# A fused Mamba block and mixture of experts on one core: the depthwise convolution of all four channel tiles as diagonal matmuls on TensorE, added onto a last tap that ScalarE writes into PSUM

## The chip, the cores and the metric

One core of one Trainium2 chip runs the whole kernel as one program. Times are device microseconds (us) of one execution. A timed figure is the median of several executions; the profile is of one further execution. The engines are named as in the profile: PE is TensorE, PEld its weight loads, DVE is VectorE, ACT is ScalarE, POOL is GpSimd, and SP issues the DMAs. L839 is line 839 of the kernel before.

## What is computed

The input has 8 sequences of 1024 tokens with 256 channels. Two layers follow each other, each inside a layer norm and a residual addition:

```
x = x + layernorm(mamba(layernorm(x)))
x = x + layernorm(moe(layernorm(x)))

mamba(x): xn = rms_norm(x) ; xb, z = split(xn @ in_proj_w)        # 256 -> 2 x 512
          xc = silu(causal_conv(xb, 4 taps, per channel) + conv_b)
          dt, B, C = split(xc @ x_proj_w) ; dt = softplus(dt @ dt_proj_w + dt_proj_b)
          h_t = exp(dt*A) * h_(t-1) + dt*B*xc ; y_t = sum_s C*h_t  # 512 channels x 16 states
          (y + xc*D) * silu(z) @ out_proj_w + residual
moe(x):   16 experts of width 128, the best 4 of them per token, within 2 of 4 groups
```

The part that matters here is the causal convolution: each of 512 channels has four weights of its own, and output `t` is `w0*x[t-3] + w1*x[t-2] + w2*x[t-1] + w3*x[t] + b`. All numbers are float32.

## The kernel before

**Chunks and groups.** The 8192 tokens are cut in 16 chunks of 512 tokens, two to a sequence. Channels lie on the 128 partitions, so the 512 inner channels make four tiles `m = 0..3`. The scan over 512 channels x 16 states of a chunk is cut in 16 groups, each of four scans (`beta`). The loop is `for p` over chunks -2 to 17 and `for g` over 16 groups (`groups()`), and every engine walks the same (p, g) in its own queue, in order. In pass p four stages run at once on different chunks: E (layer norm and transpose of chunk p+2), F (input projection, convolution, dt, B, C of chunk p+1), S (the scans of chunk p), and P with the experts (output projection, norms, routing of chunk p-1, then its experts, which begin ten groups later). E exists for 16 passes, F for p = -1 to 14, S for p = 0 to 15. The experts run beside the scans from group 10 of pass 1 on.

**One group on each engine.** DVE: the gate product of an expert (`expert_gate`, L995), scan 0 (L880), the up product (L1000), scans 1 to 3, then what the pass adds in this group, then `inputs` of the next group (L866). ACT: the exponentials `dA` of the scans (`decay`, L508, two banks, so that each waits for the scan two before it), `tanh` of an expert (L514), and the pass's own pieces between and behind them. PE: `add_states` (L448, L451), the expert's `gate` (L421) and `up` (L429), the fill of this group, `down` of an older expert (L439), and a second fill in some groups. `gate` of a group waits for DVE's gate product of the same group, which frees its bank (`m_v`); DVE's next gate product waits for `tanh`, which stands behind the decays of the next group's scans 0 and 1. POOL weighs experts (L759) and multiplies states by C (L769).

**The one shared bank.** All fills of the stages E, F and P go through a single PSUM bank, `FP`, in the fixed order of the list `FILLS`: PE fills it, ACT reads it, and PE's next fill waits for that read (`bank_free`, with the table `FREED_BY`). Input-projection fills are `b0..b3` and `z0..z3` (two matmuls each, `f_in`, L348), convolution fills `k2`, `k3` (`f_conv`, L358), `xp` (L366), `db` (`f_dt`, L373), output projection `r0`, `r1` (`p_out`, L384), transposes `xT0`, `xT1`, `x0`, `x1` (L338, L394), routing `rt`, `ct`.

**The convolution.** For each tile ACT copies the projected values to `XB` (`f_b`, L557). Tiles 0 and 1: ACT reads the bank again and writes the last tap with bias to `XC` (L561), and DVE adds the three older taps in groups 2 and 3 (`conv`, three `scalar_tensor_tensor` of 512 columns each, L839). Tiles 2 and 3: PE does four matmuls with the diagonal matrices `Kdiag`, and ACT moves the sum with bias to `XC` (`f_tap`, L568). `f_silu` (L579) follows in group 6, `f_softplus` (L598, four activations) in group 9, `f_silu_z` (L584) in group 12. Silu and softplus each take a table load before and one back to the exponential after.

**Output norm.** `p_out(0)`, `p_out(1)` run on PE in groups 2 and 3; ACT reads `r1` in the middle of group 4 (`p_rev`, L619), takes squares (L526), and DVE's `p_var` (L809) and the Newton steps `ep_newton` of group 4 wait for them.

## Time and profile before

| | |
|---|---|
| Median of 3 timed runs | 2764.61 us (2758.81 to 2765.10) |
| The profiled execution: its own time | 2764.38 us |
| The profiled execution: its span | 2762.6 us |
| Instructions | 27070 |
| Mean granted PE clock | 0.951 of full |
| POOL busy | 1474.4 us (53%) |
| DMA | 336.65 MB, mean 122 GB/s |

Busy is the time in which an engine executed something, and the share is that of the span. A row of instructions gives line, engine, operation, what it writes and reads, shapes, the number of them, then busy time, the mean of one in ns, and after the bar the engine's idle time just before them with what ended it. The mean of one includes its pipeline latency, so that back-to-back instructions start closer together than their means. In the timeline, several like instructions in a row are merged, and an idle time before them stands in brackets with its releaser.

### The profile page before, as it was taken

The page shows a single profiled execution, that of the slowest core. Times are in us where ns is not written, and L with a number is a line of the kernel's source. Part 1 is how long each engine was busy: PE and PEld are TensorE (multiplying, and loading weights), DVE is VectorE, ACT ScalarE, POOL GpSimd, SP SyncE. Part 2 cuts the span into 40 slices and gives each one's busy share as a digit, 9 for nine tenths or more (in the row PEclk, how much of TensorE's full clock was granted, in tenths as well). Part 3 has the DMA queues.
Part 4 walks back from the last instruction along what each step waited for, and adds up shares of the span by engine and source line. Part 5 has one row for each costly group of instructions (what it writes and reads, how often), then busy time and mean ns, then how long its engine had stood idle before and what let it go on. Part 6 is the DMA issues. An engine that isn't in the chain of part 4 may idle for free.

```text
span 2762.6 us, 27070 instructions
## 1 busy us (share of the span) xinstructions
PE 2426.1 (88%) x8416; PEld 1184.7 (43%) x8416; DVE 2456.4 (89%) x3265; ACT 1630.5 (59%) x3312; POOL 1474.4 (53%) x516
## 2 busy tenths in 40 slices
...
GB/s 36 229 83 116 86 179 78 179 102 143 108 133 154 100 157 102 173 83 135 152 103 160 106 173 74 150 132 107 180 82 176 97 134 120 108 172 71 69 73 59
DMA packets 164811, 336.65 MB, mean 122 GB/s; under 512 B 15771, under 2 KB 73404, under 8 KB 156220
## 3 DMA queue, kind: packets, MB, share of 16 engines
...
## 4 chain that ended last, share of the span: by engine, by line
DVE 57%; issue 15%; PE 14%; ACT 14%; DMA 0%; DVEq 0%; SPq 0%; ACTq 0%
DVE hs L880 26%; DVE hs L866 13%; DVE th L995 4%; DVE th L1000 4%; PE Gp L421 3%; PE Up L429 3%; PE MY L439 3%; PE FP L348 2%; ACT DX L526 2%; PE FP L358 1%; ACT dA L508 1%; DVE XC L839 1%; ACT L508 1%; ACT SZ L584 1%; ACT XB L526 1%
## 5 line engine op out<-in xcount | busy, mean ns | idle before, releaser
L769 POOL TENSOR_TENSOR hs<-hs,Cb 128x2048 f32<-128x2048 f32 x256 | 1158.5, 4525 | 210.0 <-DVE hs L866 210.0
L508 ACT ACTIVATE dA<-dtr,A 128x512 f32<-128x512 f32 x1024 | 702.3, 690 | 850.3 <-DVE hs L880 849.0
L759 POOL TENSOR_TENSOR th<-th,cmb 128x512 f32<-128x512 f32 x256 | 325.4, 1272 | 1061.4 <-DVE hs L866 945.3
L880 DVE TENSOR_TENSOR_SCAN hs<-dA,carry,hs 128x512 f32<-128x512 f32 x512 | 627.9, 1268 | 16.6 <-ACT dA L508 16.2
L421 PE MATMUL Gp<-x2T,Wgu 128*128 128x512 f32 x1024 | 530.8, 643 | 118.8 <-DVE th L995 118.8
L880 DVE TENSOR_TENSOR_SCAN hs<-dA,hs 128x512 f32<-128x512 f32 x512 | 597.4, 1206 | 36.6 <-ACT dA L508 35.9
L866 DVE TENSOR_TENSOR hs<-dxr,Bb 128x2048 f32<-128x2048 f32 x256 | 587.5, 2295 | 12.4 <-DMA dxr<-dx_d 12.4
L429 PE MATMUL Up<-x2T,Wgu 128*128 128x512 f32 x1024 | 493.1, 604 | 0.0
L439 PE MATMUL MY<-Wdn,th 128*128 128x256 f32 x2048 | 486.3, 380 | 0.0
L439 PEld LDWEIGHTS MY<-Wdn,th 128*128 128x128 f32 x2048 | 383.6, 190 | 136.8 <-issue 95.0
L421 PEld LDWEIGHTS Gp<-x2T,Wgu 128*128 128x128 f32 x1024 | 181.5, 196 | 452.1 <-issue 240.3
L348 PE MATMUL FP<-xT,Win 128*128 128x512 f32 x512 | 274.9, 663 | 77.5 <-ACT XB L598 41.2
L451 PE MATMUL Y<-hs,Cst 128*32 128x512 f32 x2048 | 282.0, 624 | 31.9 <-POOL hs L769 31.7
L429 PEld LDWEIGHTS Up<-x2T,Wgu 128*128 128x128 f32 x1024 | 195.3, 196 | 266.4 <-issue 222.9
L995 DVE SCALAR_TENSOR_TENSOR th<-th,Gp 128x512 f32<-128x512 f32 x256 | 174.1, 680 | 68.3 <-ACT th L514 68.3
L514 ACT ACTIVATE th<-Gp 128x512 f32<-128x512 f32 x256 | 148.3, 579 | 87.6 <-PE Gp L421 87.6
L348 PEld LDWEIGHTS FP<-xT,Win 128*128 128x128 f32 x512 | 98.1, 204 | 229.2 <-issue 99.3
L1000 DVE TENSOR_TENSOR th<-Up,th 128x512 f32<-128x512 f32 x256 | 171.0, 668 | 9.3 <-PE Up L429 8.7
L384 PE MATMUL FP<-Wout,SZ 128*128 128x256 f32 x512 | 122.8, 383 | 7.6 <-ACT DX L619 7.6
L358 PE MATMUL FP<-XB,Kdiag 128*128 128x512 f32 x256 | 122.8, 624 | 5.6 <-ACT XB L557 5.6
L384 PEld LDWEIGHTS FP<-Wout,SZ 128*128 128x128 f32 x512 | 98.2, 192 | 35.6 <-issue 15.2
L451 PEld LDWEIGHTS Y<-hs,Cst 128*32 128x32 f32 x2048 | 40.9, 109 | 159.5 <-issue 114.5
...
## 6 DMA issues: line engine op xcount, KB each, us to landing
...
dxr<-dx_d SPq DMA_DIRECT2D x128, 512.0 KB, 7.2
cmb<-cm_d SPq DMA_DIRECT2D x256, 256.0 KB, 3.6
Wdn<-in_w_dn SPq DMA_DIRECT2D x256, 128.0 KB, 3.5
...
```

The costliest lines, as they stand in the source:

```text
L348: mm = pe.matmul(FP[:, :], Win[:, q, c0:c0 + P], xT[:, q, :], start=q == 0, stop=q == KM - 1)
L421: mm = pe.matmul(Gp[:, :], Wgu[:, k, e, 0:DE], x2T[:, c % 2, k, :], start=k == 0, stop=k == KM - 1)
L429: mm = pe.matmul(Up[:, :], Wgu[:, k, e, DE:2 * DE], x2T[:, c % 2, k, :], start=k == 0, stop=k == KM - 1)
L439: mm = pe.matmul(MY[b // 2][:, (b % 2) * DM:(b % 2 + 1) * DM], th[:, q % NTH, b * P:(b + 1) * P], Wdn[:, q % NWD, :], start=e == 0 and b % ...
L451: mm = pe.matmul(Y[beta * CB:(beta + 1) * CB, :], sel_y, hs[:, G % NH, beta, :], start=False, stop=s == NSIG - 1, tile_position=(0, beta * ...
L508: act.activation(dA[h % 2][:, :], dtr[:, M % 2, beta, :], ACT.Exp, scale=A[:, k:k + 1]).then_inc(s_dA, 1)
L759: pool.tensor_tensor(th[:, q % NTH, :], th[:, q % NTH, :], cmb[:, q % 2, :], ALU.mult).then_inc(m_a, 1)
L769: pool.tensor_tensor(hs[:, G % NH, :, :], hs[:, G % NH, :, :], Cb[:, s, :].unsqueeze(1).broadcast_to([P, NBETA, CH]), ALU.mult).then_inc(s ...
L866: dve.tensor_tensor(hs[:, G % NH, :, :], dxr[:, M % 2, :, :], Bb[:, s, :].unsqueeze(1).broadcast_to([P, NBETA, CH]), ALU.mult).then_inc(s_ ...
L880: dve.tensor_tensor_scan(hv, dA[h % 2][:, :], hv, first, ALU.mult, ALU.add).then_inc(s_h, 1)
L995: dve.scalar_tensor_tensor(out=th[:, q % NTH, :], in0=th[:, q % NTH, :], scalar=1.0, in1=Gp[:, :], op0=ALU.add, op1=ALU.mult).then_inc(m_v, 1)
L1000: dve.tensor_tensor(th[:, q % NTH, :], Up[:, :], th[:, q % NTH, :], ALU.mult).then_inc(m_w, 1)
```

## The change

All four tiles take the same way. ACT copies the projected values to `XB` and then writes the last tap with bias back into the same PSUM bank. PE adds three diagonal matmuls to that (no `start` flag), and ACT copies the sum to `XC`. DVE's convolution is gone. The order of fills and their groups change: `xT0`, `xT1` from group 13 to 11, `b0` from 14 to 12, `b1` from 15 to 14, and the new `k0`, `k1` in 13 and 15; `z1` now comes ahead of `db` in group 9 and is read at the end of that group, ahead of softplus; `z2` behind `db` in group 9, `z3` in group 10; `f_z` of `z2` and `z3` both in the middle of group 10, ahead of the next decays; `f_silu_z` from group 12 to the end of group 10. `Kdiag` holds 12 matrices in place of 8, and `xd` and `cmT` share one tensor.

```
-FILLS = ['b2', 'k2', 'r0', 'r1', 'b3', 'k3', 'z0', 'xp', 'x0', 'x1', 'rt', 'db', 'z1', 'ct', 'z2', 'z3', 'xT0', 'xT1', 'b0', 'b1']
+FILLS = ['b2', 'k2', 'r0', 'r1', 'b3', 'k3', 'z0', 'xp', 'x0', 'x1', 'rt', 'z1', 'db', 'z2', 'z3', 'ct', 'xT0', 'xT1', 'b0', 'k0', 'b1', 'k1']
...
             def f_conv(p, m):
-                c = p + 1
-                bank_free(p, f'k{m}')
-                pe.wait_ge(f_act.sem, f_act.at(c, f'raw{m}'))
-                if m == PE_CONV[0] and c > 0:
+                c = p + (2 if f'k{m}' in E_FILLS else 1)
+                pe.wait_ge(f_act.sem, f_act.at(c, f'seed{m}'))
+                if c > 0:
                     pe.wait_ge(f_dve.sem, f_dve.at(c - 1, 'hist'))
-                for k in range(TAPS):
-                    mm = pe.matmul(FP[:, :], Kdiag[:, PE_CONV.index(m) * TAPS + k, :], XB[:, m, k:k + CH], start=k == 0, stop=k == TAPS - 1)
+                for t in range(HIST):
+                    mm = pe.matmul(FP[:, :], Kdiag[:, m * HIST + t, :], XB[:, m, t:t + CH], start=False, stop=t == HIST - 1, skip_group_check=True)
                 mm.then_inc(fp_full, 1)
...   (PE, the fills of a pass)
-                if F and g in (0, 4, 6, 11):
-                    f_in(p, {0: 'b2', 4: 'b3', 6: 'z0', 11: 'z3'}[g])
+                if F and g in (0, 4, 6):
+                    f_in(p, {0: 'b2', 4: 'b3', 6: 'z0'}[g])
...
                 if F and g == 9:
-                    f_dt(p)
+                    f_in(p, 'z1')
...
+                if F and g == 10:
+                    f_in(p, 'z3')
...
-                if in_e(p) and g == 13:
+                if in_e(p) and g == 11:
                     e_turn(p, 0)
-                if in_e(p) and g in (14, 15):
-                    f_in(p, f'b{g - 14}')
+                if in_e(p) and g in (12, 14):
+                    f_in(p, f'b{g // 2 - 6}')
+                if in_e(p) and g in (13, 15):
+                    f_conv(p, g // 2 - 6)
                 q = expert_at(G - 2)
                 if q is not None:
                     down(q)
...
-                if F and g in (9, 10):
-                    f_in(p, f'z{g - 8}')
-                if in_e(p) and g == 13:
+                if F and g == 9:
+                    f_dt(p)
+                    f_in(p, 'z2')
+                if in_e(p) and g == 11:
                     e_turn(p, 1)
...   (ACT)
             def f_b(p, m):
...
                 act.activation(XB[:, m, HIST:], FP[:, :], ACT.Copy).then_inc(f_act.sem, 1)
-                if m in DVE_CONV:
-                    if c >= 2:
-                        act.wait_ge(s_y, (c - 2) * GPC + m * NSIG + 1)
-                    act.activation(XC[:, c % 2, m, :], FP[:, :], ACT.Identity, scale=conv_w[:, m, HIST:HIST + 1], bias=conv_b[:, m:m + 1]).then_inc(f_act.sem, 1)
+                act.activation(FP[:, :], FP[:, :], ACT.Identity, scale=conv_w[:, m, HIST:HIST + 1], bias=conv_b[:, m:m + 1]).then_inc(f_act.sem, 1)
...
             def f_tap(p, m):
...
-                act.activation(XC[:, c % 2, m, :], FP[:, :], ACT.Identity, bias=conv_b[:, m:m + 1]).then_inc(f_act.sem, 1)
+                act.activation(XC[:, c % 2, m, :], FP[:, :], ACT.Copy).then_inc(f_act.sem, 1)
...   (ACT, middle of a group, ahead of the next decays)
-                if F and g in (10, 11):
-                    f_z(p, g - 9)
-                if in_e(p) and g == 14:
+                if F and g == 10:
+                    f_z(p, 2)
+                    f_z(p, 3)
+                if in_e(p) and g == 12:
                     e_xT(p, 1)
...   (ACT, end of a group, behind tanh)
                 if F and g == 9:
+                    f_z(p, 1)
                     f_softplus(p)
...
-                if F and g == 12:
+                if F and g == 10:
                     f_silu_z(p)
-                if in_e(p) and g == 13:
+                if in_e(p) and g == 11:
                     e_xT(p, 0)
-                if in_e(p) and g in (14, 15):
-                    f_b(p, g - 14)
+                if in_e(p) and g in (12, 14):
+                    f_b(p, g // 2 - 6)
+                if in_e(p) and g in (13, 15):
+                    f_tap(p, g // 2 - 6)
...   (DVE: conv() is taken out, and its calls)
-                if F and g in (2, 3):
-                    conv(p, g - 2)
```

## Rows read from the trace of the kernel before

**Rows 1.** The page's first part: busy us (share), instructions.
```profile
PE 2426.1 (88%) x8416; PEld 1184.7 (43%) x8416; DVE 2456.4 (89%) x3265; ACT 1630.5 (59%) x3312; POOL 1474.4 (53%) x516
```

**Rows 2.** Waits from 600 to 2400 us: us in total, times, longest.
```profile
DVE hs L880 <- ACT dA L508: 29.3, 23, 1.7
...
DVE ep_w L809 <- ACT DX L526: 16.0, 11, 1.7
```

**Rows 3.** Busy time by engine in one pass (us, count); PEclk, DMA share, GB/s.
```profile
1199.80:1359.50 159.70, 147.28 (x526) 72.49 (x526) 153.07 (x203) 101.18 (x202) 91.92 (x33) 0.98 0.38 129
```

**Rows 4.** The same columns by group, cut at DVE's gate products: groups 13, 0, 1, 2, 3.
```profile
1299.44:1310.98 11.54, 10.25 (x34) 5.13 (x34) 9.94 (x10) 8.16 (x9) 5.75 (x2) 0.76 0.68 240
...
1327.18:1335.17 7.99, 7.99 (x29) 3.82 (x28) 7.99 (x8) 4.57 (x10) 5.76 (x2) 1.00 0.97 333
1335.17:1343.63 8.46, 8.46 (x28) 3.54 (x27) 8.46 (x10) 3.94 (x8) 5.75 (x2) 1.00 0.41 136
1343.63:1353.79 10.16, 10.16 (x41) 6.00 (x40) 10.09 (x12) 6.53 (x17) 5.76 (x2) 1.00 0.12 39
1353.79:1363.96 10.17, 10.17 (x43) 6.49 (x42) 10.10 (x11) 6.19 (x19) 5.77 (x2) 1.00 0.53 183
```

**Rows 5.** The convolution's groups of instructions on DVE and ACT.
```profile
L839 DVE SCALAR_TENSOR_TENSOR XC<-XB,Cols,XC 128x512 f32<-128x512 f32 x96 | 72.3, 753 | 16.1 <-ACT XC L561 13.8
...
L557 ACT ACTIVATE XB<-FP 128x512 f32<-128x512 f32 x64 | 37.8, 590 | 30.9 <-PE FP L348 30.9
...
L561 ACT ACTIVATE XC<-FP,Cols 128x512 f32<-128x512 f32 x32 | 24.8, 775 | 0.0
...
L568 ACT ACTIVATE XC<-FP,Cols 128x512 f32<-128x512 f32 x32 | 21.9, 685 | 42.7 <-PE FP L358 42.7
```

**Rows 6.** Timeline of PE: start us, us, what, count [idle before <-releaser].
```profile
1265.68 1.98 PE L348 MATMUL FP<-xT,Win 128*128 128x512 f32 x4 [2.01 <-ACT XB L598]
...
1300.17 3.78 PE L421 MATMUL Gp<-x2T,Wgu 128*128 128x512 f32 x4 [4.14 <-DVE th L995]
...
1328.69 1.98 PE L421 MATMUL Gp<-x2T,Wgu 128*128 128x512 f32 x4
...
1336.76 1.98 PE L421 MATMUL Gp<-x2T,Wgu 128*128 128x512 f32 x4
...
1340.30 3.60 PE L358 MATMUL FP<-XB,Kdiag 128*128 128x512 f32 x8
...
1347.41 1.98 PE L421 MATMUL Gp<-x2T,Wgu 128*128 128x512 f32 x4
...
1358.08 1.98 PE L421 MATMUL Gp<-x2T,Wgu 128*128 128x512 f32 x4
```

**Rows 7.** Timeline of ACT and of DVE around group 4 of one pass.
```profile
1208.56 0.37 ACT L619 ACTIVATE DX<-FP 128x256 f32<-128x256 f32 x1
...
1211.82 0.17 DVE L809 TENSOR_SCALAR ep_w<-p_s 128x4 f32<-128x4 f32 x1 [1.44 <-ACT DX L526]
```

**Rows 8.** Timeline of ACT and of DVE at the end of group 12.
```profile
1299.45 1.28 ACT L584 ACT_TABLE_LOAD   x1
1300.74 1.91 ACT L584 ACTIVATE SZ<-SZ 128x2048 f32<-128x2048 f32 x1
...
1304.69 2.46 DVE L880 TENSOR_TENSOR_SCAN hs<-dA,carry,hs 128x512 f32<-128x512 f32 x2 [1.60 <-ACT dA L508]
```

**Rows 9.** Timeline ahead of the first scan: PE, ACT, DVE.
```profile
26.31 3.75 PE L348 MATMUL FP<-xT,Win 128*128 128x512 f32 x4 [0.78 <-ACT xT L549]
...
36.55 1.98 PE L348 MATMUL FP<-xT,Win 128*128 128x512 f32 x4 [1.35 <-ACT XC L561]
...
70.61 2.78 ACT L598 ACTIVATE XB<-FP,Cols 128x512 f32<-128x512 f32 x4
73.44 3.78 PE L348 MATMUL FP<-xT,Win 128*128 128x512 f32 x4 [4.88 <-ACT XB L598]
...
99.61 4.63 DVE L880 TENSOR_TENSOR_SCAN hs<-dA,hs 128x512 f32<-128x512 f32 x4 [9.25 <-ACT dA L508]
```

More of the change, by code:

```diff
@@ L27 @@
 NH, NTH, NWD = (3, 3, 4)
-DVE_CONV = (0, 1)
-PE_CONV = (2, 3)
 MOFF = 10
@@ L551, in f_b @@
             def f_b(p, m):
-                c = p + (2 if m in DVE_CONV else 1)
+                c = p + (2 if f'b{m}' in E_FILLS else 1)
                 act.wait_ge(fp_full, filled(p, f'b{m}'))
@@ L713, in _ @@
                 if F and g in (1, 5):
-                    f_tap(p, PE_CONV[g // 4])
+                    f_tap(p, 2 + g // 4)
                 if R_ and g in (0, 1):
@@ L725, in _ @@
                     p_ro(p)
-                if F and g in (6, 11):
-                    f_z(p, {6: 0, 11: 3}[g])
+                if F and g == 6:
+                    f_z(p, 0)
                 if F and g == 6:
@@ L785, in _ @@
                 dve.tensor_scalar(Ddiag[:, m, :], to_y, d_col[:, m:m + 1], None, ALU.mult)
-            for m in PE_CONV:
-                for k in range(TAPS):
-                    dve.tensor_scalar(Kdiag[:, PE_CONV.index(m) * TAPS + k, :], ident, conv_w[:, m, k:k + 1], None, ALU.mult)
+            for m in range(MT):
+                for k in range(HIST):
+                    dve.tensor_scalar(Kdiag[:, m * HIST + k, :], ident, conv_w[:, m, k:k + 1], None, ALU.mult)
             dve.memset(XB[:, :, 0:HIST], 0.0).then_inc(w_dve, 1)
@@ L828, in ep_newton @@
                 newton(n_dve, k, 'r', ep_w[:, :, c0:c1])
-            def conv(p, m):
-                c = p + 1
-                dve.wait_ge(f_act.sem, f_act.at(c, f'tap{m}'))
-                if m == DVE_CONV[0] and c > 0:
-                    dve.wait_ge(f_dve.sem, f_dve.at(c - 1, 'hist'))
-                xc = XC[:, c % 2, m, :]
-                for k in range(HIST):
-                    if k > 0:
-                        dve.wait_ge(f_dve.sem, f_dve.at(c, f'c{k - 1}{m}'))
-                    dve.scalar_tensor_tensor(out=xc, in0=XB[:, m, k:k + CH], scalar=conv_w[:, m, k:k + 1], in1=xc, op0=ALU.mult, op1=ALU.add).then_inc(f_dve.sem, 1)
             def keep_history(p):
                 c = p + 1
-                dve.wait_ge(f_dve.sem, f_dve.at(c, f'c{HIST - 1}{DVE_CONV[-1]}'))
-                dve.wait_ge(fp_full, filled(p, f'k{PE_CONV[-1]}'))
+                dve.wait_ge(fp_full, filled(p, f'k{MT - 1}'))
                 if c % HALVES < HALVES - 1:
```

21 lines of the change are left out of this document (10 added, 11 removed).

## The prediction, made before the changed kernel ran

> **What bounds the kernel now.** The page's first part shows DVE busy 89% of the span and PE 88% [rows 1], so shares do not decide. Next, one pass out of the even middle: 159.7 us, of which DVE is busy 153.1 and PE 147.3 [rows 3]. The waits say which of the two holds the other: over 1800 us DVE waited 29.3 us for the exponentials, mostly one wait of 0.75 and one of 1.6 a pass, and 16.0 us (1.45 a pass) for the squares of the output norm [rows 2]. DVE is the bound. But cut the pass by group and something else shows: from group 0 to group 3 PE has no idle time either [rows 4].
>
> **Lead and lag.** I follow one number: how long after DVE's gate product of a group PE starts that group's gate matmul. With PE free it is 0.73 (1300.17 against 1299.44). In group 2 it is 1347.41 - 1343.63 = 3.8, in group 3 4.3 [rows 4, 6]. PE falls behind where its groups are longer than DVE's. Plain lengths on PE, start to start: with one input projection 8.07 (1328.69 to 1336.76), with a convolution tile and the D matmul 10.65, with half the output projection 10.67 [rows 6]. A projection's two matmuls take 1.72 (half of four taps, 3.43, of the tile in [rows 6]: 0.86 a matmul), so a bare group is 6.35. DVE's lengths: 7.99 bare, 8.46 with a read of Y, 10.16 and 10.17 with the convolution [rows 4], that is 2.17 for three taps (753 ns each [rows 5], less the overlap).
>
> **The change by parts, for the 13 passes that hold everything.**
>
> 1. DVE loses 6 taps: 2 x 2.17 = -4.35 us a pass.
>
> 2. PE loses 8 matmuls and gains 12: +3.43 a pass. PE's 12.4 us of idle time [rows 3] would cover that anywhere but in the full stretch. Every tile is now three taps, 2.58. From group 13 to the end of `p_out(1)` PE has, by group: 9.80 (k0, D), 8.07 (b1), 8.93 (k1), 8.07 (b2), 9.80 (k2, D), 10.67, and in group 3 3.53 of experts plus 4.32 of projection: 63.2. With a start lag of 0.73 to 1.2 the last fill is done 64.2 after DVE's gate of group 13. ACT's read and squares then take 1211.82 - 1208.56 = 3.3 [rows 7]: `p_var` can run at 67.5. DVE alone would be there after 9.94 + 8.1 + 8.1 + 7.99 + 8.46 + 8.0 + 8.0 and 5.9 of group 4 = 64.5. So it waits 3.0 where it waited 1.44: +1.6. This is the largest loss: in groups 2 and 3 DVE's convolution filled time in which PE had the output projection. If PE's lag at group 13 were nil and its gaps zero the loss is 0.9; with 1 us more lag, 2.6.
>
> 3. `f_silu_z` leaves group 12. Its two table loads and 1.91 us cost DVE 1.60 there [rows 8], which goes: the 9.94 above has it out. At the end of group 10 the same 4.5 us stand behind `tanh` and `cmT`; DVE has the dx product and `inputs` (4.4 us) as cover. I count ACT from DVE's gate of group 10: `z3` filled 7.1, read 7.7, two decays and tanh to 9.6, `cmT` 10.2, silu with its loads 14.7, decay of scan 2 at 15.4, which DVE wants at 13.9: +1.55. Parts 1 and 3 together are then -4.4. Bounds of the relocation 0 and +3.
>
> 4. ACT gains: the tap into the bank on four tiles (was two), three tiles' worth of cheaper copies, in sum 4 x (0.59 + 0.78 + 0.59) against 2 x (0.59 + 0.78) + 2 x (0.59 + 0.69), +2.5 us [rows 5]. ACT is busy 101 of 160 [rows 3], so most lies in idle time. Where it does not: in group 4 `b3` comes late because PE lags by 8, then copy, tap and the output norm's 2.08 end 0.35 after scan 2 of group 5 wants its decay; 0.2 more in group 6; `z0` 0.35 later in group 6 ahead of silu; `e_xT(1)` 0.5 ahead of the squares of group 12: +1.4. The write of ACT into PSUM is in no row; I take it at 0.78, that of L561, from 0.59 (plain copy) to 1.3. The Trainium skill, "ScalarE: Activation LUTs", section "Step-by-step: what each stage is for", says that ScalarE writes PSUM faster than SBUF; by that each tap is somewhat shorter and the sum stands, within a few us.
>
> 5. SP: the dt store of group 10 waits 2.4 later, `cmT` 2.7; behind them are the loads of combine rows, wanted two groups (16 us) later: 0. `z1` ahead of `db` puts PE idle during softplus: 13.5 - 10.6 = 2.9 us where the same wait was 2.01 [rows 6]. PE enters group 10 with lag 1.8, covered: 0. What this costs if the clock falls is a rival below.
>
> Sum of a pass: -4.35 + 1.6 - 1.6 + 1.55 + 1.4 = -1.4; with the start lag at its low end -1.8. I take -1.6, 13 times: **-21**.
>
> **Ahead of the first scan** nothing hides anything; the first scan waits for ACT at 99.61 [rows 9]. PE runs at the lower of its two levels there for most matmuls: two take 3.75 against 1.98 [rows 9]. Four more `Kdiag` matrices +0.8. `k0` and `k1` with their reads, +5.8 and +3.4, the other two tiles -0.6, less 1 for a clock that rises sooner: +7.6. `z1` ahead of softplus: 3.8 + 0.6 + 1.1 + 0.1, less 3.0 that the norm and the table load took anyway: +2.6. After softplus (73.4) the order was z1, z2, z3, silu, xT, b0, decay = 26.2; now z2, z3, silu, xT, b0, k0, b1, decay = 28.5 to 32.4: +4.4. Sum **+15.4**, from +10 to +20. In group 15 of that pass `f_tap` of `k1` stands ahead of decays 2 and 3: **+1.2**. Pass 0 (no experts, PE at the low level much of the time): -4.35, and +4 because ACT waits in the middle of group 10 for `z3`: **-0.4**, from -4 to +4. Pass 1: **-3.5**.
>
> Total -21 + 15.4 + 1.2 - 0.4 - 3.5 = -8.3. The profiled execution took 2764.4, the median is 2764.6: **2756**.
>
> **Rivals.**
>
> *PE does not hold DVE back in groups 2 to 4.* If the lag at group 13 is small and the squares come as early as before, parts 2 and 4 cost 1.0 in all, a pass gains 3.3: 2764.4 - 43 + 12.7 = 2734. For it: PE idles 12 us a pass. Against it: none of that idle time lies in groups 0 to 3 [rows 4]. Chance 0.2.
>
> *Slower: the clock falls in the softplus gap.* After PE had waited 4.14 us for DVE in group 13, its gate matmuls took 3.78 for 1.98, and the granted clock of the group was 0.76 [rows 4, 6]; after the 2.01 in group 9 they did not [rows 6]. The new gap is 2.9. If it is enough, PE loses some 2.3 us in group 10, `z3` comes at 9.4, and ACT, which now waits for `z3` ahead of the decays of group 11, gives tanh at 12.0 where DVE wants it at 10.3: +1.75, and silu's stall grows by 0.5. That is +2.3 a pass: 2756 + 30 = 2786. It decides from the gap, somewhere between 2.01 and 4.14 us, at which the engine falls from 2.4 to 1.2 GHz; 2.9 is nearer to the lower end. Chance 0.25. The Trainium skill, "TensorE: Matmul & The Clock Gate", section "Why this matters for your kernels", advises to leave no long idle gaps between bursts of matmuls, since they bring the lower rate back. The rows of group 13 agree with it, and by it alone, with no regard to the row of 2.01, 2786 would be the forecast.
>
> *PE becomes the bound.* Then all of +3.43 a pass counts: 2764 + 45 + 15 = 2824. Idle time of 12 us a pass speaks against it. Chance 0.05.
>
> **How the numbers follow.** My forecast, most of the gain eaten by PE's full stretch, by ACT and by the prologue, has 0.5, with a range of its own from 2742 to 2770. 0.3% (8.3 us) is about what a measurement of this kernel can tell from no change. Of the 0.5, 0.25 lie below 2756.3, 0.2 within, 0.05 above; the first rival adds 0.2 to faster; the second 0.03 to same and 0.22 to slower; the third 0.05 to slower. Faster 0.45, same 0.23, slower 0.32. The range that leaves out 2 in 10 reaches from 2730 to 2788.
>
> **What would show it.** A pass of 158.0 in place of 159.7. L809's wait 3.0 a pass. PE without idle time from group 13 to 4. A DVE wait for the exponentials in group 11 of 1.5, none in group 13. The first scan at 115. ACT's row FP<-FP at 0.78. Wrong if: the lag in group 3 stays near 4; the granted clock drops in groups 9 or 10; DVE waits for tanh in group 11; the first scan comes before 108.

## The result, and the profile after

The changed kernel takes 2793.55 us, the median of 4 runs (2793.07 to 2795.52). The kernel before, on the same chip, takes 2761.74 us (4 runs, 2758.81 to 2765.1). The ratio is 1.0118, with a 95% interval of 1.0105 to 1.0131: slower by 1.2%, 32 us. The forecast was 2756, its range 2730 to 2788. The time lies above the range, in the direction of the rival "slower: the clock falls in the softplus gap", which had been priced at 2786.

The profiled execution of the changed kernel took 2795.52 us. Its page, first the busy times, then the chain that ended last:

```profile
PE 2490.6 (89%) x8544; PEld 1223.1 (44%) x8544; DVE 2390.6 (86%) x3173; ACT 1668.5 (60%) x3376; POOL 1475.2 (53%) x516
...
PE 67%; DVE 17%; ACT 12%; issue 3%; DMA 0%; SPq 0%; ACTq 0%; DVEq 0%
```

Against [rows 1], DVE lost 66 us of work and PE gained 64.5, part of it matmuls that ran at the lower clock. In spite of that neither is busier than 89% of a span that grew by 31 us, so the loss is in waits. The waits from 600 to 2400 us (us in total, times, longest), the same stretch as [rows 2]:

```profile
ACT SZ L572 <- PE FP L346: 67.8, 22, 5.4
PE FP L336 <- ACT xT L551: 45.4, 11, 4.2
DVE hs L870 <- ACT dA L510: 43.4, 36, 2.4
PE FP L346 <- ACT XB L596: 31.6, 11, 2.9
DVE ep_w L811 <- ACT DX L528: 29.6, 11, 2.9
DVE th L985 <- ACT th L516: 23.2, 11, 2.3
```

Only the rows that begin with DVE are time lost by the bound engine. Its wait for the exponentials went from 29.3 to 43.4 us, its wait for the squares from 16.0 to 29.6, and a wait for `tanh` that the kernel before doesn't have at all costs 2.1 us in each of 11 passes. The first row says whom ACT itself waited for: for the fills of `z`, 5.4 us at the longest. The fourth is PE's idle time under softplus, 2.87 us in each of 11 passes.

Where in a pass? The table gives each group's mean length over passes 3 to 13, cut at DVE's gate products, of both kernels. It averages the two kinds of pass, which differ by 2.0 us before.

| group | 0 | 1 | 2 | 3 | 4 | 5 | 6 | 7 | 8 | 9 | 10 | 11 | 12 | 13 | 14 | 15 | pass |
|---|---|---|---|---|---|---|---|---|---|---|---|---|---|---|---|---|---|
| before | 8.05 | 8.58 | 10.26 | 10.26 | 12.47 | 9.72 | 10.51 | 9.05 | 8.06 | 15.39 | 10.25 | 8.04 | 11.25 | 11.49 | 8.04 | 8.05 | 159.47 |
| after | 8.05 | 8.58 | 8.05 | 8.33 | 13.66 | 9.89 | 10.96 | 9.21 | 8.05 | 15.39 | 12.44 | 10.39 | 11.74 | 9.72 | 8.05 | 8.05 | 160.53 |

Groups 2 and 3 give 4.14 us, as they should. Groups 10 and 11 take 4.54 back. The windows of the changed kernel, one pass, columns as in [rows 3] and [rows 4]: groups 2, 3, 4, then 9, 10, 11, 12, 13.

```profile
1204.90:1213.00 8.10, 8.10 (x31) 4.26 (x31) 8.10 (x9) 5.31 (x13) 5.75 (x2) 1.00 0.14 49
1213.00:1221.28 8.28, 8.28 (x36) 5.21 (x35) 8.17 (x9) 4.77 (x14) 5.79 (x3) 1.00 0.40 121
1221.28:1234.92 13.64, 13.64 (x53) 8.40 (x52) 10.69 (x25) 8.48 (x28) 5.74 (x2) 1.00 0.39 140
...
1273.16:1288.61 15.45, 12.58 (x48) 6.61 (x48) 14.63 (x40) 9.37 (x13) 5.75 (x2) 0.89 0.15 51
1288.61:1300.97 12.36, 11.67 (x35) 4.86 (x34) 10.38 (x9) 4.20 (x8) 7.66 (x4) 0.86 0.16 59
1300.97:1311.38 10.41, 7.45 (x32) 3.73 (x30) 8.21 (x7) 9.12 (x14) 3.88 (x1) 1.00 0.57 179
1311.38:1323.17 11.79, 10.65 (x36) 5.00 (x40) 10.25 (x21) 8.94 (x25) 5.76 (x2) 0.86 0.16 57
1323.17:1333.00 9.83, 9.73 (x36) 4.55 (x32) 9.83 (x10) 4.87 (x8) 5.75 (x2) 1.00 0.78 279
```

Read the column of the granted clock, the third from the end: 0.89 in group 9 and 0.86 in group 10. (The 0.86 in group 12 lies behind another gap of PE, the wait for the read of `xT1` in the second row of the waits; the kernel before has its fall in group 13.) In the same pass of the kernel before both groups have 1.00, and group 10 takes 10.31:

```profile
1254.29:1269.73 15.44, 13.41 (x57) 6.13 (x55) 14.62 (x40) 8.77 (x12) 5.76 (x2) 1.00 0.28 98
1269.73:1280.04 10.31, 8.62 (x36) 3.91 (x32) 10.31 (x10) 4.24 (x7) 5.74 (x2) 1.00 0.02 4
```

PE's timeline of the changed kernel across the same place:

```profile
1282.86 1.12 PE L370 MATMUL FP<-xd_cm,SelDt 33*128 33x512 f32 x2
1286.86 3.78 PE L346 MATMUL FP<-xT,Win 128*128 128x512 f32 x4 [2.87 <-ACT XB L596]
1290.43 1.83 PE L445 MATMUL Y<-XC,Ddiag 128*128 128x512 f32 x2
...
1293.19 1.98 PE L418 MATMUL Gp<-x2T,Wgu 128*128 128x512 f32 x4
...
1296.72 1.88 PE L346 MATMUL FP<-xT,Win 128*128 128x512 f32 x4
```

The profile lists each of these float32 matmuls as two records: x4 are the two matmuls of an input fill, x2 is one D matmul, x6 are three matmuls. `z1` stands ahead of `db` now, so nothing is left for PE while ACT computes softplus. It idles 2.87 us, and `z2` then takes 3.78 for 1.98, the D matmul 1.83 for 1.02. The clock is at its upper level at the start of the gap and at the lower of the two, 0.50, from 1286.00 to the end of `z2`:

```profile
1286.86:1290.64 3.78, 3.78 (x5) 1.71 (x6) 3.78 (x4) 1.37 (x2) 1.87 (x2) 0.50 0.74 277
```

The gate matmul of group 10 starts at 1293.19, 4.6 after DVE's gate product at 1288.61. The fill of `z3` (1296.72) ends at 1298.6. ACT and DVE behind it:

```profile
1298.64 0.60 ACT L572 ACTIVATE SZ<-FP 128x512 f32<-128x512 f32 x1 [5.14 <-PE FP L346]
1299.13 1.29 ACT L510 ACTIVATE dA<-dtr,A 128x512 f32<-128x512 f32 x2
1300.36 0.58 ACT L516 ACTIVATE th<-Gp 128x512 f32<-128x512 f32 x1
...
1302.86 1.92 ACT L582 ACTIVATE SZ<-SZ 128x2048 f32<-128x2048 f32 x1
```
```profile
1300.97 0.69 DVE L985 SCALAR_TENSOR_TENSOR th<-th,Gp 128x512 f32<-128x512 f32 x1 [1.99 <-ACT th L516]
...
1306.82 2.46 DVE L870 TENSOR_TENSOR_SCAN hs<-dA,carry,hs 128x512 f32<-128x512 f32 x2 [2.20 <-ACT dA L510]
```

ACT stood still for 5.14 us in the middle of its busiest place, because it executes its queue in order and the read of `z3` is written ahead of two decays and `tanh`. DVE waits 1.99 us for `tanh`, and 2.20 in group 11 for the decay behind silu.

### The profile page after: what moved, and what is told of

It reads as the page before. It is cut to its first block, busy times and chain, and to the rows that moved or that the text cites. A ratio compares the mean times of both kernels' runs of the same rounds, so it can differ in the third digit from the quotient of the medians.

```text
span 2793.7 us, 27307 instructions
## 1 busy us (share of the span) xinstructions
PE 2490.6 (89%) x8544; PEld 1223.1 (44%) x8544; DVE 2390.6 (86%) x3173; ACT 1668.5 (60%) x3376; POOL 1475.2 (53%) x516
## 4 chain that ended last, share of the span: by engine, by line
PE 67%; DVE 17%; ACT 12%; issue 3%; DMA 0%; SPq 0%; ACTq 0%; DVEq 0%
PE Gp L418 14%; PE Up L426 12%; PE MY L436 11%; PE FP L346 8%; DVE hs L870 7%; PE Y L448 6%; PE FP L355 5%; DVE hs L856 5%; PE FP L381 4%; PE FP L363 2%; PE Y L445 2%; ACT dA L510 2%; ACT XB L596 2%; ACT DX L528 1%; ACT SZ L582 1%
## 5 line engine op out<-in xcount | busy, mean ns | idle before, releaser
L418 PE MATMUL Gp<-x2T,Wgu 128*128 128x512 f32 x1024 | 520.5, 632 | 49.4 <-DVE th L985 48.8
L426 PE MATMUL Up<-x2T,Wgu 128*128 128x512 f32 x1024 | 484.4, 595 | 0.0
L346 PE MATMUL FP<-xT,Win 128*128 128x512 f32 x512 | 285.2, 685 | 55.0 <-ACT XB L596 46.2
L448 PE MATMUL Y<-hs,Cst 128*32 128x512 f32 x2048 | 294.1, 648 | 24.4 <-POOL hs L771 24.2
L355 PE MATMUL FP<-XB,Kdiag 128*128 128x512 f32 x384 | 188.5, 629 | 15.8 <-ACT FP L560 15.7
L346 PEld LDWEIGHTS FP<-xT,Win 128*128 128x128 f32 x512 | 106.2, 215 | 209.4 <-issue 128.5
L355 PEld LDWEIGHTS FP<-XB,Kdiag 128*128 128x128 f32 x384 | 76.6, 203 | 122.7 <-issue 93.1
L381 PEld LDWEIGHTS FP<-Wout,SZ 128*128 128x128 f32 x512 | 98.8, 193 | 33.7 <-issue 15.2
```

The source lines that it names most:

```text
L346: mm = pe.matmul(FP[:, :], Win[:, q, c0:c0 + P], xT[:, q, :], start=q == 0, stop=q == KM - 1)
L355: mm = pe.matmul(FP[:, :], Kdiag[:, m * HIST + t, :], XB[:, m, t:t + CH], start=False, stop=t == HIST - 1, skip_group_check=True)
L381: pe.matmul(o, SZ[:, c % 2, m, b * P:(b + 1) * P], Wout[:, m, :], start=m == 0, stop=False)
L418: mm = pe.matmul(Gp[:, :], Wgu[:, k, e, 0:DE], x2T[:, c % 2, k, :], start=k == 0, stop=k == KM - 1)
L426: mm = pe.matmul(Up[:, :], Wgu[:, k, e, DE:2 * DE], x2T[:, c % 2, k, :], start=k == 0, stop=k == KM - 1)
L448: mm = pe.matmul(Y[beta * CB:(beta + 1) * CB, :], sel_y, hs[:, G % NH, beta, :], start=False, stop=s == NSIG - 1, tile_position=(0, beta * ...
```

## The experiments

Twelve kernels were run. The table shows all with the mean pass and, where it matters, the lag: how long after DVE's gate product PE starts the gate matmul of the same group, as the prediction counts it (all means over passes 3 to 13).

| kernel | us (median) | ratio to before, 95% | pass | lag in 10 | length 10 | 11 | 3 | 4 |
|---|---|---|---|---|---|---|---|---|
| before | 2761.7 | | 159.47 | 1.08 | 10.25 | 8.04 | 10.26 | 12.47 |
| after | 2793.55 | 1.0118 (1.0105 to 1.0131) | 160.53 | 4.65 | 12.44 | 10.39 | 8.33 | 13.66 |
| 1 `db` before `down` | 2753.59 | 0.9966 (0.9955 to 0.9978) | 157.46 | 1.19 | 10.25 | 9.37 | 8.47 | 13.66 |
| 2 gap filled | 2762.83 | 1.0000 (0.9991 to 1.0010) | 158.30 | 2.06 | 10.25 | 9.98 | 8.69 | 13.64 |
| 3 `z3` read late | 2763.51 | 1.0007 (0.9998 to 1.0017) | 158.61 | 3.81 | 10.25 | 10.65 | 8.33 | 13.66 |
| 4 reorder alone | 2807.01 | 1.0162 (1.0147 to 1.0178) | 162.16 | 4.26 | 12.05 | 10.24 | 10.26 | 12.47 |
| 5 two tiles seeded | 2760.07 | 0.9992 (0.9982 to 1.0001) | 159.60 | 0.87 | 10.25 | 8.04 | 10.26 | 12.52 |
| 6 a tap less | 2724.73 | 0.9860 (0.9846 to 0.9875) | 155.52 | 1.73 | 10.26 | 9.73 | 8.05 | 12.49 |
| 7 ACT's order | 2738.12 | 0.9909 (0.9894 to 0.9924) | 156.67 | 1.18 | 10.25 | 8.04 | 9.41 | 13.66 |
| 8 first scan early | 2733.29 | 0.9891 (0.9876 to 0.9905) | 156.67 | 1.18 | 10.25 | 8.05 | 9.42 | 13.66 |
| 9 `xT1` first | 2746.34 | 0.9940 (0.9927 to 0.9952) | 157.82 | 1.18 | 10.25 | 8.05 | 9.59 | 13.66 |
| 10 DVE convolution, new order | 2751.67 | 0.9964 (0.9950 to 0.9977) | 158.21 | 1.26 | 10.25 | 8.05 | 10.26 | 12.48 |
| 11 gap of 13 filled | 2726.86 | 0.9864 (0.9849 to 0.9879) | 155.97 | 1.19 | 10.25 | 8.05 | 8.31 | 13.64 |
| 12 before, gap filled | 2762.94 | 1.0003 (0.9994 to 1.0011) | 159.47 | 1.08 | 10.25 | 8.04 | 10.26 | 12.47 |

**The theory** after the result: the gap under softplus drops PE's clock, PE enters group 10 with a lag of 4.6 for 1.8, and ACT's wait for `z3` hands the lag on to DVE, twice. **Rivals**: the gap itself costs, whatever the clock; or the reorder is fine and the convolution with its tap in PSUM is what PE or ACT can't carry.

**1. Shorten the gap.** In group 9, PE does `f_dt` ahead of `down` instead of behind it.

```diff
 if F and g == 9:
     f_in(p, 'z1')
+    f_dt(p)
...
 if F and g == 9:
-    f_dt(p)
     f_in(p, 'z2')
```

> From the changed kernel: in group 9 the dt broadcast comes ahead of the expert's down matmuls instead of behind them, nothing else. Theory (the idle stretch of PE during softplus, 2.87 us, drops its clock, and ACT then waits in order for z3 in group 10): the gap shrinks to about 1.3 us, the granted clock stays at its upper level in groups 9 and 10, PE enters group 10 with a lag near 1.0 in place of 4.65, group 10 falls from 12.4 to 10.3 us, group 11 from 10.4 to 9.7, a pass loses 2.8 us, 2793 becomes about 2756. Rival (what costs is where silu of z and the reads of z stand on ACT, the clock is beside the point): group 10 keeps 11.5 or more, time 2780 or more.

Measured: 2753.59 us, ratio to before 0.9966. The move of a single matmul takes 40 us off the changed kernel. Groups 9 and 10 by windows, then PE's timeline:

```profile
1255.17:1270.61 15.44, 13.71 (x52) 6.74 (x51) 14.61 (x41) 9.37 (x13) 5.77 (x2) 1.00 0.23 73
1270.61:1280.90 10.29, 9.52 (x37) 4.15 (x40) 10.29 (x9) 5.19 (x9) 5.75 (x2) 1.00 0.11 39
```
```profile
1267.99 1.98 PE L346 MATMUL FP<-xT,Win 128*128 128x512 f32 x4 [1.05 <-ACT XB L596]
1269.82 1.02 PE L445 MATMUL Y<-XC,Ddiag 128*128 128x512 f32 x2
```

The gap is 1.05, the clock stays at 2.4 GHz (1.00), the lag is 1.19, and DVE's wait for `tanh` is gone. This fits the theory, but it shortens the gap and removes the fall together, and lets `z2` start earlier.

**2. Keep the dependences, hold the clock.** PE executes three matmuls with zero weights behind `f_dt`, from pass 2 on; they add zero to an open bank, so the output is the same.

```diff
 f_dt(p)
+if p >= 2:
+    for _ in range(3):
+        pe.matmul(MY[0][:, :], Zero[:, :], Win[:, 0, 0:CH], start=False, stop=False, skip_group_check=True)
 f_in(p, 'z2')
...
+dve.memset(Zero[:, :], 0.0)
```

> From the changed kernel: behind the dt broadcast PE does three more matmuls of 512 columns with zero weights onto the experts' bank (they add nothing), which fill 2.6 of the 2.87 us in which it waits for softplus; no dependence and no order is changed. Theory of the clock: no drop in groups 9 and 10, lag at group 10 about 1.8, group 10 at 10.3, group 11 at 9.7, time about 2757 although PE does more. Rival (order of the reads alone): z2 starts when it did, so groups 10 and 11 stay within 0.3 us of 12.4 and 10.4 and the time stays at 2790 or above.

Measured: 2762.83 us, 6 more than expected (the profiled execution, at 2758.08, was the fastest of ten). `z2` starts no earlier than in the changed kernel, 13.7 us into group 9 in both, since it still waits for ACT's last softplus read, and yet:

```profile
1257.52:1272.96 15.44, 15.34 (x56) 7.69 (x56) 14.62 (x41) 9.37 (x13) 5.75 (x2) 1.00 0.17 51
1272.96:1283.26 10.30, 9.61 (x35) 4.27 (x33) 10.30 (x10) 4.70 (x8) 5.78 (x2) 1.00 0.18 69
```
```profile
1268.27 2.84 PE L495 MATMUL MY<-Win,Zero 128*128 128x512 f32 x6
...
1271.21 1.98 PE L347 MATMUL FP<-xT,Win 128*128 128x512 f32 x4
```

`z2` takes 1.98 again and group 10 10.30. A kernel that gives PE more to do is 31 us faster than the changed one, so the gap alone is not the cost, the fall of the clock in it is. The lag is 2.06 where the prediction had 1.8 for a gap without a fall: that step's own arithmetic was sound. Silu's stall is 1.9 here (group 11: 9.98 for 8.04) and 1.3 in experiment 1, whose lag is 0.9 less.

**3. Keep the fall, take ACT's wait away.** ACT reads `z3` behind `tanh`.

```diff
 if F and g == 10:
     f_z(p, 2)
-    f_z(p, 3)
...
 tanh(q)
+if F and g == 10:
+    f_z(p, 3)
```

> From the changed kernel: ACT reads z3 behind tanh of group 10 instead of ahead of the next decays. Theory: DVE no longer waits for tanh (2.0 us), group 10 falls to 10.3 although PE's clock still drops; cmT and silu move behind the late z3, so DVE's wait for the exponentials in group 11 grows from 2.2 to 3 or more: a pass gains about 1.3 us, 2776. Rival (the drop costs through PE's own queue, not through ACT's wait for z3): no gain, 2790.

Measured: 2763.51 us, 13 us better than expected. Group 10, then DVE in group 11:

```profile
1269.59:1279.89 10.30, 9.61 (x31) 3.82 (x30) 10.30 (x10) 4.51 (x8) 5.76 (x2) 0.95 0.19 71
```
```profile
1285.59 2.46 DVE L871 TENSOR_TENSOR_SCAN hs<-dA,carry,hs 128x512 f32<-128x512 f32 x2 [2.06 <-ACT dA L510]
```

The clock still falls in this pass (0.95 in group 10), the lag is 3.8 in the mean, and group 10 takes 10.30 in this pass and 10.25 in the mean, as in the kernel before: the wait for `tanh` came through ACT's order alone. The silu stall did not grow to the 3 us or more that I had expected; it is 2.06 in this pass, 2.6 in the mean (10.65 for 8.04), where the changed kernel has 2.35. The mean mixes two things. Here `z2` took its full 3.78 in only 5 of the 11 passes, and in those group 11 takes 11.4 to 12.0, a stall of 3.4 to 3.9 as expected. In the pass of the window above it took 3.37. In two passes the clock did not fall at all behind the same gap, and group 11 takes 8.9:

```profile
951.52 1.98 PE L346 MATMUL FP<-xT,Win 128*128 128x512 f32 x4 [2.88 <-ACT XB L596]
```

So each pass of this trace shows the price of the fall by itself, 2.5 to 3.1 us in group 11 when it is whole. That is one part of the 13 us. The other is ahead of the even middle: at the start of pass 2 this kernel is 8.1 us ahead of the changed one (4.9 of them at the first scan), and the expectation had counted nothing there.

**4. The reorder alone**: the kernel before with its own convolution (three taps on DVE for tiles 0 and 1, four on PE for 2 and 3) and the new order of fills, reads and `f_silu_z`.

```diff
-FILLS = [..., 'rt', 'db', 'z1', 'ct', 'z2', 'z3', 'xT0', ...]
+FILLS = [..., 'rt', 'z1', 'db', 'z2', 'z3', 'ct', 'xT0', ...]
...
 if F and g == 9:
-    f_dt(p)
+    f_in(p, 'z1')
...
-if F and g == 12:
+if F and g == 10:
     f_silu_z(p)
```

> From the kernel before: only the new order and places of the fills and of the silu of z; the convolution stays as before, two tiles on DVE and two with four taps on PE. Theory (the reordering, not the convolution, is what costs): groups 10 and 11 grow by 4.4 us together, groups 12 and 13 lose 1.2, a pass is 3.2 us longer than before, the first scan some 6 us later: about 2808, slower than the whole change. Rival (PE's additional taps and ACT's writes are the cost): within 10 us of the kernel before, 2762 to 2772.

Measured: 2807.01 us, as expected. Group 10 of one pass (12.05 in the mean):

```profile
1288.30:1299.73 11.43, 10.74 (x35) 4.71 (x34) 10.38 (x9) 4.23 (x8) 6.74 (x3) 0.93 0.17 65
```

The reorder alone costs 2.7 us a pass (162.16 for 159.47), more than the whole change; the convolution on top of it brings 1.6 back (160.53). So the rival that blames the convolution falls.

**5. The tap in the bank on tiles 2 and 3 alone**, in the kernel before: ACT's Identity writes tap and bias over the fill in the bank and three matmuls add to it, where four matmuls had started the bank anew.

```diff
-    for k in range(TAPS):
-        mm = pe.matmul(FP[:, :], Kdiag[:, PE_CONV.index(m) * TAPS + k, :], XB[:, m, k:k + CH], start=k == 0, stop=k == TAPS - 1)
+    for k in range(HIST):
+        mm = pe.matmul(FP[:, :], Kdiag[:, PE_CONV.index(m) * HIST + k, :], XB[:, m, k:k + CH], start=False, stop=k == HIST - 1, skip_group_check=True)
...   (ACT, f_b)
+                else:
+                    act.activation(FP[:, :], FP[:, :], ACT.Identity, scale=conv_w[:, m, HIST:HIST + 1], bias=conv_b[:, m:m + 1]).then_inc(f_act.sem, 1)
```

> From the kernel before: only tiles 2 and 3 get their last tap from ACT through PSUM and three diagonal matmuls in place of four; DVE keeps tiles 0 and 1, no order is changed. Theory: PE has 1.7 us a pass less in groups 1 and 5, but DVE's wait in group 4 is ACT's reading order there (1.44), so a pass stays within 0.3 us of 159.4 and the time within 5 us of the kernel before; the write of ACT into PSUM takes 0.74 and delays nobody. Rival (the ACT round trip through PSUM costs by itself): more than 5 us slower.

Measured: 2760.07 us, ratio 0.9992 (0.9982 to 1.0001), no difference that can be told. The write into PSUM costs no more than one into SBUF: here and in the changed kernel, by groups of instructions,

```profile
L563 ACT ACTIVATE FP<-FP,Cols 128x512 f32<-128x512 f32 x32 | 23.8, 743 | 0.0
```
```profile
L560 ACT ACTIVATE FP<-FP,Cols 128x512 f32<-128x512 f32 x64 | 47.5, 742 | 0.0
```

against the 775 ns of L561 in [rows 5].

**6. What does PE's full stretch still hold back?** From experiment 1, the oldest tap is left out on all four tiles, so that the convolution has two matmuls for three. This kernel does not compute the reference; it serves as a measurement alone.

```diff
-for t in range(HIST):
+for t in range(1, HIST):
```

> From e1_dt_before_down: the oldest tap is left out of all four tiles, two matmuls for three (the output leaves out that part of the convolution). Theory (PE's full stretch from group 13 to group 4 delays the output norm's squares and with them DVE): 3.4 us less on PE in the stretch, so group 4 falls from 13.66 to about 12.5, where ACT's order holds it as in the kernel before, group 6 from 10.95 to 10.5; a pass gains 1.6 us, 2730. Rival (ACT's additional reads and writes hold groups 4 and 6): both groups stay within 0.2 us, 2748 or more.

Measured: 2724.73 us, 29 us less than experiment 1. The wait for the squares (us in total, times, longest) is what it was in [rows 2]:

```profile
DVE ep_w L811 <- ACT DX L528: 16.0, 11, 1.7
```

Group 4 takes 12.49 for 13.66 and group 3 8.05 for 8.47 in experiment 1. So the price of group 4 in the changed kernel is PE's full stretch from group 13 on, as part 2 had it.

**7. ACT's order.** From experiment 1: `z3` and silu right behind `tanh` with the turned weights behind them, the read of `xT0` ahead of `z_my`, and in group 12 the squares ahead of the read of `xT1`.

```diff
     tanh(q)
+if F and g == 10:
+    f_z(p, 3)
+    f_silu_z(p)
...
-if in_e(p) and g == 12:
-    e_xT(p, 1)
 if g == 12 and 0 <= p - 2 < NC:
     z_squares(p - 2)
+if in_e(p) and g == 12:
+    e_xT(p, 1)
...
```

> From e1_dt_before_down: ACT reads z3 and does the silu of z right behind tanh of group 10, cmT behind it; in group 11 it reads xT0 ahead of the experts' sums; in group 12 it takes the squares ahead of xT1. Theory (these are waits in ACT's queue only): group 11 falls from 9.4 to about 8.1, group 12 from 11.7 to 11.2, PE's gap of 4.1 us in group 11 shrinks below 2 and its clock stays up; a pass 155.5, time about 2730. Rival (cmT and the sums, now later, hold the combine loads, POOL and PE): the gain is eaten, 2750 or more.

Measured: 2738.12 us, 15 less than experiment 1 and 8 more than expected. Groups 11 and 12 came out as expected (8.04 and 11.25), PE's gap in group 11 shrank from 3.9 to 1.2 in the mean, and group 3 got worse, 9.41 for 8.47. The reason stands in group 12, in PE's timeline:

```profile
1291.35 2.99 PE L346 MATMUL FP<-xT,Win 128*128 128x512 f32 x4 [2.16 <-ACT xT L551]
```

A gap of 2.16, an input fill in 2.99 for 1.95, and PE enters group 13, where its full stretch begins, with a lag of 1.95 for 0.9 in the mean. Nothing in that stretch gives it back: it arrives in group 3. Passes 10 and 11 of the same trace are the counter-test. There the clock did not fall behind this gap, the lag at group 13 is 0.74 for 2.2, and group 3 of the next pass takes 8.25 and 8.38, where it takes 9.61 to 9.72 in the other passes from 3 to 13.

**8. The first scan.** From experiment 7, ACT issues the first eight decays between the reads of the second chunk's fills ahead of pass 0. The first four:

```diff
...   (ACT, middle of a group)
+if p == -1 and g == 12:
+    decay(0)
+    decay(1)
...   (ACT, end of a group)
 if in_e(p) and g in (12, 14):
     f_b(p, g // 2 - 6)
+if p == -1 and g == 12:
+    decay(2)
+    decay(3)
...
```

> From e7_act_order: in the pass before the first scans ACT issues the decays of the first two groups between the fills of the second chunk instead of behind them. Theory (ACT's queue order, not data, holds the first scan from 98 to 111 us): first scan at about 99, time 10 to 12 us below e7, about 2719. Rival (the fills of the second chunk then come late for pass 0 and the time is lost again there): less than 4 us below e7.

Measured: 2733.29 us, 4.8 less than experiment 7, where 10 to 12 had been expected; that is nearer to the rival. The first scan starts at 96.5 for 111.7, but in the third group, group 2 of pass 0, DVE waits (its timeline):

```profile
117.75 2.34 DVE L882 TENSOR_TENSOR_SCAN hs<-dA,hs 128x512 f32<-128x512 f32 x2 [6.72 <-ACT dA L510]
```

Of the 15.2 us that were won, 6.3 are left one group later and 5.6 at the end. The decays of that group stand behind ACT's reads of `k1` and `b2`, and for these fills ACT itself waits for PE, 4.63 and 1.98 us. So the rest is held by PE's fills through ACT's order, and moving decays alone does not win it.

**9. `xT1` first again.** From experiment 8, the read of `xT1` ahead of the squares.

```diff
+if in_e(p) and g == 12:
+    e_xT(p, 1)
 if g == 12 and 0 <= p - 2 < NC:
     z_squares(p - 2)
-if in_e(p) and g == 12:
-    e_xT(p, 1)
```

> From e8_first_scan_early: in group 12 ACT reads xT1 ahead of the squares again. Theory (e7 gave back 1.1 us in group 3, because the late read of xT1 let PE enter its full stretch with a lag of 1.9 in place of 0.8): lag at group 13 near 0.8, group 3 from 9.4 to 8.4, group 12 from 11.2 to 11.7, a pass gains 0.55, 2726. Rival (the longer group 3 has another cause): group 3 stays at 9.4, group 12 grows, 2738.

Measured: 2746.34 us, 13 slower than experiment 8 where 7 faster was expected. PE's timeline and window in group 13:

```profile
1295.23 3.78 PE L418 MATMUL Gp<-x2T,Wgu 128*128 128x512 f32 x4 [2.81 <-DVE th L997]
```
```profile
1294.50:1304.33 9.83, 9.10 (x15) 3.85 (x16) 9.83 (x11) 4.38 (x7) 5.73 (x2) 0.66 0.79 279
```

The lag at the gate of group 13 is 0.74, as wanted. But PE is now so early that it waits 2.81 us for DVE, and the clock falls at the very start of the full stretch. The lag in group 14 is 2.85, group 1 takes 9.12 and group 3 9.59, where experiment 11, without the fall, has 8.59 and 8.31.

**10. The good order with the convolution left on DVE**: the kernel before with the orders of experiments 1 and 7, and `xT1` ahead of the squares. Two of the places, against experiment 4:

```diff
 if F and g == 9:
     f_in(p, 'z1')
+    f_dt(p)
...
     tanh(q)
+if F and g == 10:
+    f_z(p, 3)
+    f_silu_z(p)
...
```

> From e4_reorder_alone (convolution as in the kernel before, tiles 0 and 1 on DVE): the order of e1 and e7 on PE and ACT, with xT1 read ahead of the squares. Theory (the convolution on PE and the order of ACT's queue are worth about the same): groups 10 and 11 at 10.2 and 8.1, groups 2, 3 and 4 as in the kernel before, a pass 158.2, time about 2745, so that the convolution on PE is worth some 14 us less than its 57 us of DVE time under either order. Rival (with a good order the convolution on PE is worth nothing more): within 5 us of e9.

Measured: 2751.67 us, 158.21 a pass; the pass is as expected, the time 7 more. So a good order is worth 1.3 us a pass to the kernel before too. Experiment 9 is only 5.3 us faster, 0.4 a pass, which is at the edge of the rival's "within 5 us"; experiment 11 decides. Group 13 here, in the one pass with the deepest fall:

```profile
1297.82:1307.65 9.83, 9.09 (x18) 4.44 (x18) 9.83 (x10) 4.42 (x7) 5.75 (x2) 0.65 0.80 279
```

In this pass the clock falls as in experiment 9 (0.65 for 0.66). Over the 11 passes the falls are milder (0.86 in the mean, three passes without any, for 0.78). But here they cost nothing: passes with and without a fall are equally long (159.16 to 159.19 and 157.03 to 157.06 us, by kind), and group 3 has the 10.26 of the kernel before. With the convolution on DVE, group 13 has no `k0`, the lag is down to 0.78 by group 14, and nobody has waited for it.

**11. Fill the gap of group 13.** From experiment 9, three zero-weight matmuls ahead of the gate matmul of group 13, from pass 2 on.

```diff
+if in_e(p) and p >= 2 and g == 13:
+    for _ in range(3):
+        pe.matmul(MY[0][:, :], Zero[:, :], Win[:, 0, 0:CH], start=False, stop=False, skip_group_check=True)
 if q is not None:
     gate(q)
```

> From e9_xT1_first, which has a gap of 2.81 us on PE ahead of the gate matmul of group 13, a granted clock of 0.66 in that group and a lag of 3 us one group later: three matmuls with zero weights in that gap, on the experts' bank. Theory (the clock falls in that gap, and the lag that it leaves is carried through the full stretch into group 3): the clock of group 13 at 1.00, lag at group 14 about 0.8, group 3 from 9.4 to 8.4, a pass of 156.0 to 156.9, time about 2722. Rival (the lag of group 14 comes from k0 or its wait for the tap, not from the clock): lag stays at 2.6 or more, 2744.

Measured: 2726.86 us, ratio to before 0.9864 (0.9849 to 0.9879), 5 more than expected. It is the fastest kernel here that computes the whole reference, 1.4% faster than the kernel before and 67 us faster than the changed one. PE's timeline and group 13:

```profile
1285.70 2.84 PE L460 MATMUL MY<-Win,Zero 128*128 128x512 f32 x6
...
1288.59 1.98 PE L419 MATMUL Gp<-x2T,Wgu 128*128 128x512 f32 x4
```
```profile
1287.86:1297.68 9.82, 9.78 (x30) 4.55 (x32) 9.82 (x10) 4.86 (x8) 5.75 (x2) 1.00 0.82 277
```

The clock is 1.00 and group 3 takes 8.31. Against experiment 10, which has the same orders from pass 2 on but for the filler, the convolution on PE is worth 2.2 us a pass (155.97 for 158.21), where on top of the changed kernel's order it was worth 1.6 and without the filler 0.4.

**12. The same filler in the kernel before**, four matmuls in its gap of 4.14 us of [rows 6].

```diff
+if in_e(p) and p >= 2 and g == 13:
+    for _ in range(4):
+        pe.matmul(MY[0][:, :], Zero[:, :], Win[:, 0, 0:CH], start=False, stop=False, skip_group_check=True)
 if q is not None:
     gate(q)
```

> From the kernel before, which has a gap of 4.1 us at the same place in every pass and a granted clock of 0.76 in group 13: four matmuls with zero weights in it. Theory (a fall of the clock costs only where PE's lag then reaches another engine; in the kernel before it is worked off by group 14): the clock of group 13 rises to 1.00 and the time stays within 3 us of 2762. Rival (each fall costs what PE loses, about 2.3 us a pass): 2735.

Measured: 2762.94 us against 2762.8, ratio 1.0003 (0.9994 to 1.0011). The gate fill takes 1.98 for 3.78, and the pass stays at 159.47. The clock of group 13 did not rise to the 1.00 that was expected, but from 0.80 to 0.96 in the mean. In the pass of [rows 6], later in the same group:

```profile
1307.64 1.12 PE L339 MATMUL FP<-Cst,xin 128*128 128x128 f32 x4 [2.83 <-ACT xT L553]
```

A second gap, of 2.83, drops the clock there instead (0.89 for the group, 0.76 in [rows 4]). In 5 of the 11 passes neither group 13 nor 14 has a fall at all, and the passes are as long as the others of their kind, to within 0.2 us: the falls of the kernel before harm nobody.

## Why the prediction was wrong

**The step that failed** is this one of part 5: "PE enters group 10 with lag 1.8, covered: 0". The gap was forecast at 2.9 and is 2.87. But in that gap the clock fell, in all 11 passes between 600 and 2400 us: the lag is 4.65, not 1.8, and it is not covered, since ACT's read of `z3` waits for it. Groups 10 and 11 take 2.19 and 2.35 more than before, where the forecast had 0 and 1.55. Experiment 2 shows the share of the clock with all dependences kept: 2.2 a pass (160.53 against 158.30); experiment 3 shows the way that the loss takes to DVE.

**The rival that came true** had the chain right: the fall, `z3` late, ACT waiting ahead of the decays, `tanh` late. It had `z3` at 9.4 us into the group and +1.75 at `tanh`; measured were 10.0 (1298.64 - 1288.61) and 1.99. It had +2.3 a pass; without the fall the pass is 157.46 to 158.30, with it 160.53, so 2.2 to 3.1. Its 2786 is 8 us short of 2793.55, so the top of the range at 2788 was too. Its chance of 0.25 was what was wrong, and the evidence behind it was thin: "after the 2.01 in group 9 they did not" rests on one pass. The same place of the kernel before in five other passes, PE's timeline:

```profile
628.15 2.91 PE L348 MATMUL FP<-xT,Win 128*128 128x512 f32 x4 [2.02 <-ACT XB L598]
...
1105.96 2.85 PE L348 MATMUL FP<-xT,Win 128*128 128x512 f32 x4 [1.87 <-ACT XB L598]
...
1584.45 3.47 PE L348 MATMUL FP<-xT,Win 128*128 128x512 f32 x4 [2.02 <-ACT XB L598]
...
2062.20 3.35 PE L348 MATMUL FP<-xT,Win 128*128 128x512 f32 x4 [1.89 <-ACT XB L598]
2221.93 2.67 PE L348 MATMUL FP<-xT,Win 128*128 128x512 f32 x4 [2.01 <-ACT XB L598]
```

In 5 of the 12 passes between 600 and 2400 us the clock does fall behind a gap of 1.87 to 2.02, and behind the gaps of 4.01 to 4.15 in group 13 it falls in 11 of 11. Read over all passes, the trace of before said that a gap of 2.9 would more likely drop it than not; then 2786 would have been the forecast. The Trainium skill, "TensorE: Matmul & The Clock Gate", section "Why this matters for your kernels", warns of long idle gaps between bursts of matmuls. The trace agrees with it, with the 3.78 us of `z2` behind each gap of 2.87.

**The terms**, per pass, against what the groups show:

| step | forecast | measured |
|---|---|---|
| 1. DVE's six taps (groups 2, 3) | -4.35 | -4.14 after; group 2 -2.21, group 3 -1.93, the rest lost to PE's lag of 5.7 |
| 2. wait for the squares (group 4) | +1.6, wait 3.0 | +1.19, wait 2.7 (29.6 / 11) |
| 3. silu out of group 12's end (group 13) | -1.60 | -1.77 |
| 3. silu into group 10's end (group 11) | +1.55 | +1.33 in experiment 1, +2.35 after |
| 4. ACT's extra work (groups 5, 6, 7, 12) | +1.4 | +0.17, +0.45, +0.16, +0.49: +1.27 |
| 4. the tap's write to PSUM | 0.78 | 0.742 |
| 5. the softplus gap (group 10) | 0 | +2.19 |
| a pass | -1.6 | +1.06 after, -2.0 in experiment 1 |

With the clock up (experiment 1) the other terms held to within some 0.4 us each. There a pass gains 2.0, and the whole kernel comes to 2753.59 against a forecast of 2756. So the sum comes close for a kernel that differs from the changed one by the place of one matmul, in part by luck, as the prologue shows below. Of the prediction's four signs of being wrong two came: the clock drops in groups 9 and 10, and DVE waits for `tanh` in group 11. The lag in group 3 did not stay near 4 (it is 5.7), and the first scan, at 111.58, did not come before 108.

**The first pass and what is ahead of it.** The first scan starts at 111.58:

```profile
111.58 4.57 DVE L870 TENSOR_TENSOR_SCAN hs<-dA,hs 128x512 f32<-128x512 f32 x4 [13.03 <-ACT dA L510]
```

That is 12.0 later than [rows 9], for +15.4, within the bounds +10 to +20. Passes 0 and 1, with the tap in group 15, then add 0.6, for -2.7. In both, DVE's six taps give 4.5 and groups 10 and 11 take more than that back, 5.3 and 5.5; for pass 0 the prediction had 4 of it, from the wait for `z3`, and for pass 1 it had a net gain of 3.5. At the start of pass 2 the sum is +12.6, for +12.7: two misses that cancel. Pass 2 takes 163.7 for 159.7, a loss of 4.0 for a gain of 1.6 in the forecast. PE enters it with a lag of 5.1 where later passes begin with 1.8; groups 1 and 3 take 10.31 and 9.84, where later passes have 8.59 and 8.33, and in group 1 DVE waits 1.75 for a decay that stands behind ACT's read and write of `b2`. Every other kernel here with three taps on all four tiles has the same lag and the same two groups; in experiment 6, with two taps, the lag is 3.6 and they take 9.00 and 8.98. So the loss follows the lag that PE brings into the pass; where pass 1 gets it from was not tested. Passes 3 to 13 add 11 x 1.06 = 11.7, passes 14 and 15 1.2, and what follows to the last gate product 1.7. Together 31.2, against 2795.52 - 2764.38 = 31.1 of the two profiled executions.

**The other rivals.** "PE does not hold DVE back in groups 2 to 4" falls: the wait for the squares nearly doubles, and experiment 6 takes it back by giving PE less to do. "PE becomes the bound" falls too: in the pass from 1204.90 to 1365.00 PE is idle for 9.05 of 160.1 us; its share of the chain, 67%, comes from the places where DVE has slack. That the change doesn't do what it says can be ruled out: the convolution's row on DVE is gone.

**What stays open**: where PE's lag at the start of pass 2 comes from; why the clock falls behind a gap of 2.88 in 9 of 11 passes of experiment 3 and in 11 of 11 of the changed kernel; what the prologue would allow if PE's fills came earlier there and not only the decays (experiment 8). No experiment kept the clock up in the changed kernel's order ahead of pass 2.
